# Graph network on one core: attention masks made by TensorE in PSUM instead of ScalarE in SBUF

## The reference, cut to what matters

```python
for i in range(4):
    Q = _ln(h @ Wq[i], gq[i], bq[i]);  K = _ln(h @ Wk[i], gk[i], bk[i])
    score = (Q[src] * K[dst]).sum(-1) + 0.1 * (edge_attr * Q[src][:, :40]).sum(-1) + logm[dst]
    smax = segment_max(score, src)                      # largest score of each source node
    es = exp(minimum(score - smax[src], 20.0))
    alpha = es / (segment_sum(es, src)[src] + 1e-10)
    aggi = segment_sum(alpha[:, None] * (h[dst] @ Wm[i]), src)
    h = _ln(h + leaky(concat([h, aggi]) @ Wu[i]), go[i], bo[i])
```

## Time and profile before

| | |
|---|---|
| runs, median (3) | 15027.07 us (15020.17 to 15038.46) |
| profiled execution, its own time | 15085.92 us |
| its span, first to last instruction | 15084.2 us |
| busy: TensorE matmul, VectorE, ScalarE, GpSimd | 75%, 81%, 56%, 50% |
| granted TensorE clock, mean over the span | 0.587 |

### The profile page before, as it was taken

One profiled execution on the slowest core, in us unless ns is written; L12 is line 12 of the kernel. 1 busy time (PEld: TensorE's weight loads), 2 busy tenths in 40 slices (PEclk: granted clock), 3 DMA queues, 4 the chain that ended last, 5 costly groups with the idle time before them and its releaser, 6 DMA issues. The chain is left out here.

```text
span 15084.2 us, 633523 instructions
## 1 busy us (share of the span) xinstructions
PE 11381.7 (75%) x194575; PEld 9646.2 (64%) x194575; DVE 12169.1 (81%) x29602; ACT 8505.6 (56%) x28744; POOL 7505.2 (50%) x9217
## 2 busy tenths in 40 slices
PE   3677777764666688879888888888886667676576
PEld 3455555543566687768777877777776666676566
DVE  7566666655789889988998889988998778699986
ACT  0444444434567678867887688867885202067630
POOL 3455555543445455536554555545552454565445
PEclk5555555555775675558555955586555657585585
DMA  9322222246589677748775777757776856579856
GB/s 377 92 62 63 63 64 64 63 53 110 193 276 284 212 267 189 189 130 301 187 189 149 280 191 187 188 209 220 185 185 191 270 168 200 149 280 281 224 200 169
DMA packets 3519407, 2773.01 MB, mean 184 GB/s; under 512 B 2341177, under 2 KB 3123128, under 8 KB 3519018
## 3 DMA queue, kind: packets, MB, share of 16 engines
q1 hardware_dynamic: 2793946, 1087.59, 28.4%
q0 software_dynamic: 236192, 860.68, 19.4%
q10 hardware_dynamic: 489008, 821.78, 14.7%
HBM read 1656.63 MB, written 1112.41 MB: 184 GB/s over the span
## 5 line engine op out<-in xcount | busy, mean ns | idle before, releaser
L1327 PE MATMUL ps<-arena 128*128 128x49 bf16 x56160 | 2729.6, 218 | 1021.9 <-DVE arena L1838 494.6
L1327 PEld LDWEIGHTS ps<-arena 128*128 128x128 fp8e4 x56160 | 2456.4, 119 | 1353.3 <-issue 1351.2
L1294 PE MATMUL ps<-block_tables,arena 128*128 128x98 bf16 (+2 forms) x56160 | 2451.0, 201 | 558.6 <-DVE arena L1808 273.6
L1294 PEld LDWEIGHTS ps<-block_tables,arena 128*128 128x128 bf16 (+1 forms) x56160 | 2218.7, 99 | 791.5 <-issue 413.9
L777 POOL COPY block_tables<-arena 128x294 bf16 (+2 forms) x2340 | 1427.4, 610 | 2198.7 <-PE ps L1294 1321.6
L738 POOL DMA_INDIRECT edge_records<-arena x1563 | 1635.6, 1046 | 1329.1 <-ACT arena L893 887.6
L970 ACT ACTIVATE arena<-ps 128x392 f32<-128x392 f32 (+1 forms) x3900 | 1710.4, 480 | 1023.1 <-PE ps L1294 611.2
L761 POOL DMA_INDIRECT arena<-chunk_layer_rows,map_a x1040 | 1066.0, 1025 | 2094.1 <-ACT arena L1034 2005.4
L1034 ACT ACTIVATE arena<-arena,small 128x49 f32<-128x49 f32 x8320 | 1996.9, 323 | 104.5 <-ACT small L1026 6.0
L1808 DVE TENSOR_SCALAR arena<-arena,iota_row 128x1024 bf16<-128x1024 uint8 x2080 | 1565.3, 753 | 111.3 <-PE ps L1294 50.9
L1822 DVE TENSOR_TENSOR arena<-arena 128x392 f32<-128x392 f32 x2340 | 1358.0, 580 | 355.2 <-PE ps L1327 309.5
(11 more groups left out here) (332 smaller groups left out, 20298.4 us busy)
## 6 DMA issues: line engine op xcount, KB each, us to landing
chunk_layer_rows<-arena ACTq DMA_DIRECT2D x1040, 392.0 KB, 3.3
arena<-node_hot_a SPq DMA_DIRECT2D x1820, 128.0 KB
arena<-edge_hot_a SPq DMA_DIRECT2D x1560, 128.0 KB
chunk_gated<-arena ACTq DMA_DIRECT2D x520, 324.0 KB, 2.6
arena<-edge_records SPq DMA_DIRECT2D x1040, 160.0 KB
chunk_rows<-arena ACTq DMA_DIRECT2D x780, 196.0 KB, 1.9
arena<-edge_records SPq DMA_DIRECT2D x520, 196.0 KB
arena<-edge_hot_b SPq DMA_DIRECT2D x780, 128.0 KB
```

The source lines that it names most:

```text
L1294: last = pe.matmul(psv[:, 2 * r + j // tpb, (j % tpb) * w:(j % tpb + 1) * w], hot[:, s, j * P:(j + 1) * P], bt4[:, s, i, 0:w], start=i == ...
L1327: last = pe.matmul(to[s % 2], he4j[:, s % 4, j, :], low_part(i, s, j), start=j == 0 and i == 0, stop=j == C8 - 1 and i == 2)
```

## The change

ScalarE's mask instruction goes, with its tile and its counter `at["not"]`. TensorE writes the mask into banks 4 and 5 itself, ahead of the spread scores: for each bank one matmul of 512 columns writes -1e30 everywhere (`big_off`, whose first row is -1e30, times a matrix of ones) and a second adds 1e30 times the one-hot (`big_on`, a scaled identity). The spreading matmuls then add the scores onto it. The peak becomes a plain `tensor_reduce` over the two banks. The wait for the previous peak stands ahead of the masks now, and TensorE's turn runs sums, next query, masks (lag 1), turning, picks of the maximum, spreading. SyncE's load of the one-hot waits only for the picks.

```diff
@@ act: attend @@
-                def masks(k, s):
-                    if isinstance(k, int) and k < 4:
-                        hold(act, "act", (ht_loaded[s % 4], landed(l + 1, k, s, 4)))
-                    else:
-                        hold(act, "act", (ht_loaded[s % 4], landed(l + 1, k, s, 4)), (at["gm"], base + k - 3))
-                    act.activation(hn4[:, s % 4, :], hs4[:, s % 4, :], ACT.Identity, bias=neg_big[:, 0:1], scale=BIG).then_inc(at["not"], 1)
...
-                walk(nc, act, NS, [(2, weights), (2, weigh), (1, READ), (0, masks), (1, corrected, True), (0, turn), (1, kept, True)], (ACT_ENGINE, blk_a))
+                walk(nc, act, NS, [(2, weights), (2, weigh), (1, READ), (1, corrected, True), (0, turn), (1, kept, True)], (ACT_ENGINE, blk_a))
@@ pe: attend @@
+                def mask_s(k, s):
+
+                    again(pe, at["gm"], base, k, 1)
+                    for h in range(2):
+                        pe.matmul(psv[:, 4 + h, :], big_off, all_ones, start=True, stop=False, skip_group_check=True)
+                        pe.matmul(psv[:, 4 + h, :], big_on, hs4[:, s % 4, h * 512:(h + 1) * 512], start=False, stop=False, skip_group_check=True)
+
                 def spread_s(k, s):
                     r = s % 2
                     pe.wait_ge(at["ev"], base + k + 1)
-                    again(pe, at["gm"], base, k, 1)
                     for j in range(C8):
                         last = pe.matmul(psv[:, 4 + j // 4, (j % 4) * P:(j % 4 + 1) * P], sel[:, j * P:(j + 1) * P],
-                                         s_turn[:, r * P:(r + 1) * P], start=True, stop=True)
+                                         s_turn[:, r * P:(r + 1) * P], start=False, stop=True, skip_group_check=True)
...
-                walk(nc, pe, NS, [add_up(l + 1, l + 1, ps_att, parts, 4), (0, pick_query), (1, turn_s), (2, pick_max), (1, spread_s)])
+                walk(nc, pe, NS, [add_up(l + 1, l + 1, ps_att, parts, 4), (0, pick_query), (1, mask_s), (1, turn_s), (2, pick_max), (1, spread_s)])
@@ dve: start-up, attend @@
-            dve.memset(neg_big[:, :], -BIG).then_inc(cleared, 1)
+            dve.memset(all_ones, 1.0).then_inc(cleared, 1)
...
+            do(dve.tensor_scalar(big_on, ident[:, :], BIG, None, ALU.mult))
+            do(dve.memset(big_off, 0.0))
+            do(dve.memset(big_off[0:1, :], -BIG))
...
-                    hold(dve, "dve", (at["bc"], base + k + 1), (at["not"], base + k + 1))
-                    dve.tensor_tensor_reduce(out=junk[:, :], in0=ps[:, 4 * 512:6 * 512], in1=hn4[:, s % 4, :],
-                                             scale=1.0, scalar=-BIG, op0=ALU.add, op1=ALU.max, accum_out=gm[:, r:r + 1]).then_inc(at["gm"], 1)
+                    hold(dve, "dve", (at["bc"], base + k + 1))
+                    dve.tensor_reduce(gm[:, r:r + 1], ps[:, 4 * 512:6 * 512], AX.X, ALU.max).then_inc(at["gm"], 1)
@@ sp: load_node_hots @@
-                    if masked is not None and not (isinstance(k, int) and k < 4):
-                        hold(sp, "sp", (at["not"], masked * NS + k - 3))
```

More of the change, by code:

```diff
@@ L207, in build @@
         hot_n = main(4 * BT // 2, BF16)
-        junk = main(BT // 2, BF16)
+        spare = main(BT // 2)
+        junk = spare[:, 0:P // 2].bitcast(BF16)
+        all_ones = spare[:, P:P + 256].bitcast(BF16)
+        big_off = spare[:, P + 256:P + 320].bitcast(BF16)
+        big_on = spare[:, P + 320:P + 384].bitcast(BF16)
         scratch = arena[:, scratch_at:scratch_at + NB * 2 * WK]
@@ L250, in build @@
         half_pi = sb("half_pi", [P, 1])
-        neg_big = sb("neg_big", [P, 1])
         blk_of = sb("block_of_partition", [P, 2])
@@ L357, in build @@
         he4j = hot_e.bitcast(F8).rearrange("p (s j c) -> p s j c", s=4, c=P)
-        hn4 = hot_n.rearrange("p (s c) -> p s c", s=4)
         rows8g = edges(arena[:, scratch_at:], 8, WG)
@@ L434, in build @@
         at = {n: sem("att_" + n) for n in (
-            "q", "keys", "not", "prod", "red", "mid", "tr", "ev", "bc", "gm", "max", "low", "cor",
+            "q", "keys", "prod", "red", "mid", "tr", "ev", "bc", "gm", "max", "low", "cor",
             "sub", "exp", "ph")}
@@ L636, in load_edges, with load_node_hots @@
                 return step
-            def load_node_hots(kbp_no, masked=None):
+            def load_node_hots(kbp_no):
                 def step(k, s):
                     hold(sp, "sp", (ht_used, kbp_no * NS + k - 3))
-                    if masked is not None and not (isinstance(k, int) and k < 4):
-                        hold(sp, "sp", (at["not"], masked * NS + k - 3))
                     sp.dma_start(hs4u[:, s % 4, :], hot_na[bass.ds(k * P, P), :]).then_inc(ht_loaded[s % 4], 16)
@@ L679, in layer @@
                 spread(l + 1, row_b)
-                walk(nc, sp, NS, [(0, load_node_hots(l * 2 + 3, l)), (0, load_edges(0, R, at["keys"], l * NS)), (2, load_edge_hots(hot_ea, l + 1))])
+                walk(nc, sp, NS, [(0, load_node_hots(l * 2 + 3)), (0, load_edges(0, R, at["keys"], l * NS)), (2, load_edge_hots(hot_ea, l + 1))])
             with sp.Fori(0, L - 1) as l:
```

## The result

| | before | after |
|---|---|---|
| time, median (lowest to highest), 4 runs each | 15031.11 us (15020.17 to 15038.46) | 15129.15 us (15111.87 to 15152.31) |
| profiled execution | 15085.92 us | 15142.03 us |
| mean granted clock | 0.587 | 0.706 |
| four attention walks, first to last peak | 4573.6 us | 4636.3 us |

The ratio is 1.0063, with a 95% interval of 1.005 to 1.0076. The forecast was 14,907 us and faster; the range held the time, the sign was wrong. The two profiled executions are 56 us apart, the medians 98 us, because the profiled one of before stands 55 us above its median. The walks differ by 63 us, so all of it is in the walks, as the forecast assumed.

What follows compares the result with a forecast made beforehand. VectorE was taken to bound the attention walks; its floor falling 4.27 to 4.20 us and less TensorE lateness gave 0.115 us x 1040 steps = 120 us, hence 14,907 us at a held 2.4 GHz clock; range 14,780 to 15,330.

Steps and rivals of the forecast that it cites:

- part 3: TensorE's clock level in the attention walks: held at 2.4 GHz, with 5568 columns in a step of 4.30 us.
- part 4: TensorE's work a step at 2.4 GHz: 3.1 to 3.4 us under VectorE's 4.2, 0.8 us or more to spare.
- the clock alternates: Rival, chance 0.17: TensorE's clock switches levels in the walks; step 4.7 us, +300 us, 15,325 us.
- about a quarter of the time: Share of low-clock time above which low spells take more than TensorE's spare time gives back.
- The sum for a held clock: Attention walks at 2.4 GHz: step 4.30 us, gain 120 us, 14,907 us; high clock and faster had 0.66.
- part 6: VectorE's peak as plain maximum: about 1220 ns, read saves 0, one wait and one increment fewer save 0.07 us a step.
- the lateness: TensorE's late input to the peak: falls from 0.04 us a step (0.26 in walk 4) to about 0.02.
- part 5: Wait for the previous peak moves from spreading to masks: over first, its loop some 3.5 us, shorter than the step.
- Part 1: ScalarE loses one 1.13 us instruction a step: buys nothing itself; about 0.25 us of the spreading's lateness goes.
- Part 2: TensorE gains four 512-column matmuls a step: 1.7 to 2.24 us at 1.2 GHz, 0.87 to 1.06 at 2.4 GHz.
- the stretched subtractions: VectorE's two subtractions run longer than in a quiet step: 0.08 us a step, forecast to stay.
- VectorE is the bound: Attention walks: VectorE sets the step, TensorE about 0.2 us behind; VectorE's floor goes from 4.27 to 4.20 us.

Runs made afterwards that it cites:

- e1: Changed kernel plus two 512-column matmuls a step ahead of the query's picks, into the bank these overwrite: 14989.39 us, 0.9937 of the kernel before.
- e6: e1 with ScalarE's mask instruction of the kernel before put back, its product unused: 14943.85 us, 0.9942 of the kernel before.
- e4: Changed kernel with the masks issued right ahead of the spreading instead of ahead of the turning: 16800.18 us, 1.1159 of the kernel before.
- f1: The kernel before, unchanged, profiled on the second chip, where it takes 13926.18 us: ratio 0.9999.
- e8: Changed kernel with each bank's first mask matmul issued twice, two more 512-column matmuls a step: 15037.25 us, 1.0003 of the kernel before.

## Why the prediction was wrong, point by point

**The step that failed** is the choice in part 3, "I take: held at 2.4 GHz". It rested on an average, 5568 columns in 4.30 us, set against a stretch of another kind of work, and on 1026 columns a microsecond outside the masks being "nearer" to the row that held. The trace of after shows 0.88 to 0.92 in the walks and 28 to 41 falls in each. e1 shows it as the cause: two more matmuls a step, and the falls are gone, with 195 us of walk time. The part named the right danger, the lumps, and the right evidence, a stretch at 0.69 with pauses of 0.91 us. In after the pause before a fall shown above is 0.93. I had computed TensorE's spare time (0.8 us or more) in part 4 and counted it as cover only; on this engine it is what puts the clock at risk.

On the Trainium skill ("TensorE: Matmul & The Clock Gate", its table of goals: the high level is lost when TensorE idles long between bursts): the trace disagrees with it as I had read it, since the clock fell with no pause longer than 1.1 us in the walks of after. In e1, with few pauses over 0.5, it held.

**The rival that came true** is *the clock alternates*, at 0.17. Its mechanism was right, its price too high: 4.7 us a step forecast, 4.48 measured (4636.3/1036), +63 us in the walks and +98 by the medians, not +300. A step at 1.2 GHz was forecast at 5.5 us in full; the slow ones measured 4.8 to 5.6 (those shown 5.0 and 5.1), since the clock is back within two steps, and 27% of the steps are slow. The clock is low for 24% of walk 1 (a mean of 0.88), where I had 62% before the spare time pays back. The rival's own border, "about a quarter of the time", is near where it came out.

**The sum for a held clock was right in total, and part of that is luck.** e1 is that case, measured: 4.287 us a step (4441.1/1036) for 4.30 forecast, 132 us off the walks for 120. Its ratio on 15,031 is 14,936 us, within the case's own range of 14,780 to 14,980. But its terms were off and cancel. From before to e1 (means in 5600 to 6600) the idle time at the peak fell from 0.18 to 0.03 us, 0.15 where 0.09 was forecast (part 6 and the lateness); the two subtractions lost 0.08, where nothing was forecast; and 0.13 came back as the wait of the first subtraction for the picks (0.06 to 0.19), with 0.02 more ahead of the products. That wait the sum put at nothing: part 5 followed the way from the masks over the spreading to the peak, and not the shorter one from the masks over turning and picks to the first subtraction. It is also where the low clock costs its time: in after the same wait is 0.38 us a step.

- Part 1, *ScalarE*: its copy of the turned scores follows the turning at once (turning 6414.19, copy 6414.52 in after). It is worth nothing that can be told (e6), as forecast, for a held clock.
- Part 2, *Four masks*: 0.22 apart at the high level (0.88 us for four, forecast 0.87 to 1.06), 0.40 to 0.43 at the low (1.75, forecast 1.7 to 2.24). The fp8 operand costs no more. The 0.86 us by the Trainium skill ("TensorE: Matmul & The Clock Gate", "Back-to-back issue gap") agrees with the 0.88.
- Part 4, *TensorE's work at 2.4 GHz* under VectorE's step: right, and this was the trouble.
- Part 5, *The moved wait*: "it is over first" was true of before's timing. After, the masks reach it early and stop, 217 times in 260 steps, 0.62 us on average. What it costs is the picks' place behind it, as said above. The e4 run shows the value of the place chosen.
- Part 6, *The peak*: 1225 ns as forecast, and the read was hidden, as taken. The wait and the increment were priced at 0.07; the gap ahead of the peak shrank by twice that, from 0.16 us to 0.01 (medians of walk 1), on chip A. The 0.15 was given as the upper bound.
- The sum, *the stretched subtractions* "stay": wrong and small. The second has a mean of 570 ns for 628 before, 0.06 us less a step.

**VectorE is the bound**, I wrote, with a floor of 4.20 us. On chip B its step is 3.93 with the same instructions, so 0.3 us of that floor were gaps that I counted as fixed: those ahead of the first subtraction and of the products, which on chip A stand behind the late counter of the picks. In the quiet step of the earlier trace rows, too, the subtraction starts 0.11 us after that counter, so VectorE was not alone in setting the 4.27. The trace of one chip could not show that these gaps shrink on another. There before's walks are hardly faster than on A (4499.7 for 4573.6), because TensorE at 1.2 GHz, with the 4.28 us of its own cycle, takes VectorE's place as the bound: the peak waits 222.1 us for the spreading in f1. So the change is worth more there, 266 us of walk.

## What to carry to other kernels

When a change moves TensorE to its high clock, TensorE gets slack, and the slack can lose the clock again: forecast the falls by the pauses and lumps of the new order, not by its mean work, and give that case the larger chance when the trace has a lumpy stretch that alternated. When work moves ahead of others in a queue, follow every consumer behind it, not the longest way alone: here it was the one-column picks that came late. The cheapest test is a matmul or two of 512 columns into a bank that is about to be overwritten; here they cost nothing, since the engine was waiting, and on chip A brought 0.6% below before in place of 0.6% above it. A ratio near 1 from one chip may be another on the next (1.0063 and 0.9806 for the same pair), so look at which engine has the last 0.2 us there.

The version that beats both kernels is after with fillings: 0.9937 with two on chip A; 0.9756 with one on chip B, where after has 0.9806. One filling was not run on a chip of the slower kind.

## What the runs showed of the hardware that I had not expected

- Two Trainium2 chips run the same program 8% apart (15,031 and 13,926 us). The larger part lies ahead of the first walk, which starts at 5494.2 us on one and 4651.3 on the other. In 1500 to 1600, all engines and then clock and DMA, first the kernel before on chip A, then on B:

```profile
1500.00:1600.00 100.00, 74.72 (x412) 50.60 (x411) 64.31 (x151) 47.39 (x196) 57.18 (x54) 0.50 0.23 63
```

```profile
1500.00:1600.00 100.00, 99.45 (x561) 68.46 (x560) 86.02 (x200) 61.60 (x253) 78.06 (x73) 0.50 0.32 84
```

 Every engine does a quarter less on A at the same clock. There ScalarE stands still for 3.9 us until 1500.6 and VectorE for 4.4 until 1502.1, and the record names no transfer for it, only "remote"; TensorE then waits 3.4 us for VectorE, until 1507.3. The cause was not found.
- A counter that TensorE raises can stand well behind the matmul: for the picks of the maximum 0.36 us (e1), 0.40 (before) and 0.33 (e6) behind the modelled end on chips of kind A, for the turning 0.46 in e5. It is 0.01 for both in every kernel on chip B, and for the picks in e4 and e8. The cause is open.
- A fall of the clock costs about 1.3 us here on both chips, although the engine runs at half speed for some 7 us (6403 to 6410 in the timeline above): most of it is taken up by the slack.
- A plain maximum over 1024 float32 columns of PSUM takes 1225 ns, exactly what the fused add and maximum took with a second operand.
